# Mamba and additive-attention kernel: one planned order for all engines, built by list scheduling instead of by shares of a phase

## The reference

```python
# 1. mamba, per sample: L = 4096 tokens, 256 inner channels, 16 states
xh, z = split(x @ W_in);  xh = silu(causal_conv_k2(xh));  dt = softplus((xh @ W_x)[:8] @ W_dt + b_dt)
h[t] = exp(dt[t] * A) * h[t-1] + dt[t] * B[t] * xh[t];  y[t] = <h[t], C[t]> + D * xh[t]
x = x + silu(group_norm((y * silu(z)) @ W_out))
# 2. additive attention, causal (strictly below the diagonal), 16 hidden units a
s[i, j] = sum_a w2[a] * tanh(f[i, a] + g[j, a] + b1[a]) + b2;  w = exp(s) masked / its row sum;  t = t + w @ ln(t)
# 3. a layer of 64 experts, each taking its top 8 tokens of a sample out of softmax over tokens of the gate
```

## Time and profile before

| what | us |
|---|---|
| median of 2 runs | 15874.43 (15864.13 to 15884.73) |
| the profiled execution | 15875.92 |
| span of its instructions | 15874.2 |
| first attention tanh starts | 1208.2 |
| one period (sample 4, first exponential of one scan to that of the next) | 1866.5 |

### The profile page before, as it was taken

One profiled execution on the slowest core, in us unless ns is written; L12 is line 12 of the kernel. 1 busy time (PEld: TensorE's weight loads), 2 busy tenths in 40 slices (PEclk: granted clock), 3 DMA queues, 4 the chain that ended last, 5 costly groups with the idle time before them and its releaser, 6 DMA issues.

```text
span 15874.2 us, 128485 instructions
## 1 busy us (share of the span) xinstructions
PE 10063.1 (63%) x51338; PEld 3010.7 (19%) x51338; DVE 8213.9 (52%) x10768; ACT 9981.7 (63%) x6475; POOL 443.8 (3%) x536
## 2 busy tenths in 40 slices
PE   2126556766667666676667666676666766677775
PEld 0001111211122111221122211221112211122223
DVE  5763556355554555455554555645555455542133
ACT  1114566566766666566675666666675766788991
POOL 0000000000000000000000000000000000000000
PEclk6558788888888888888888888888888888889996
DMA  4541554134422445134441344314442244400005
GB/s 147 173 145 68 141 130 120 45 119 125 129 80 76 118 121 126 55 100 114 123 113 41 112 124 125 88 69 114 123 129 65 90 112 123 122 21 32 22 15 195
DMA packets 551062, 1624.30 MB, mean 102 GB/s; under 512 B 49272, under 2 KB 49920, under 8 KB 547904
## 3 DMA queue, kind: packets, MB, share of 16 engines
q1 hardware_dynamic: 550464, 1616.08, 35.4%
HBM read 1368.44 MB, written 247.46 MB: 102 GB/s over the span
## 4 chain that ended last, share of the span: by engine, by line
DMA 28%; PE 27%; ACT 26%; DVE 12%; issue 4%; SPq 2%; POOL 1%; DVEq 0%; POOLq 0%; ACTq 0%
ACT arena L1333 19%; DMA arena<-dt_scratch 17%; PE banks L710 14%; DMA arena<-dx_scratch 8%; PE banks L729 4%; DVE arena L978 3%; ACT arena L1341 3%; ACT arena L1350 2%; ACT arena L1312 2%; DVE arena L1116 1%; PE banks L645 1%; PE banks L741 1%; PE banks L657 1%; PE banks L605 1%; PE banks L686 1%
## 5 line engine op out<-in xcount | busy, mean ns | idle before, releaser
L710 PE MATMUL banks<-arena,w2b 128*32 128x512 f32 (+4 forms) x36864 | 6541.0, 649 | 3707.3 <-ACT arena L1333 2073.8
L1333 ACT ACTIVATE arena<-arena 128x2048 f32<-128x2048 f32 (+15 forms) x4096 | 7011.7, 1785 | 329.5 <-PE banks L710 274.5
L1312 ACT ACTIVATE arena<-arena,An 128x1024 f32<-128x1024 f32 x1024 | 1173.0, 1146 | 3341.3 <-DMA arena<-dt_scratch 3340.4
L710 PEld LDWEIGHTS banks<-arena,w2b 128*32 128x32 f32 x36864 | 1600.5, 122 | 8378.3 <-ACT arena L1333 4255.8
L978 DVE TENSOR_TENSOR_SCAN arena<-arena 128x1024 f32<-128x1024 f32 x1024 | 2386.2, 2330 | 0.0
L969 DVE TENSOR_TENSOR arena<-arena 128x1024 f32<-128x1024 f32 x1024 | 1251.2, 1222 | 1684.1 <-DMA arena<-dx_scratch 1683.0
L1130 DVE TENSOR_TENSOR arena<-arena,banks 128x512 f32<-128x512 f32 (+1 forms) x512 | 334.2, 653 | 2331.2 <-PE banks L729 2331.1
L645 PE MATMUL banks<-arena,sel 128*32 128x512 f32 x4096 | 761.1, 682 | 921.1 <-DVE arena L992 731.1
L992 DVE TENSOR_TENSOR arena<-arena 128x1024 f32<-128x1024 f32 x1024 | 1232.5, 1204 | 152.3 <-DMA arena<-bc_scratch 152.3
L729 PE MATMUL banks<-arena 128*128 128x512 f32 (+3 forms) x2304 | 1080.0, 590 | 70.8 <-POOL arena L1408 31.5
L1341 ACT ACTIVATE arena<-arena 128x1024 f32<-128x1024 f32 (+7 forms) x512 | 1058.3, 2117 | 90.6 <-DVE arena L1116 88.8
(11 more groups left out here) (169 smaller groups left out, 5127.5 us busy)
## 6 DMA issues: line engine op xcount, KB each, us to landing
arena<-dt_scratch SPq DMA_DIRECT2D x1024, 512.0 KB
arena<-dx_scratch SPq DMA_DIRECT2D x1024, 512.0 KB
xc_scratch<-arena SPq DMA_DIRECT2D x64, 512.0 KB, 2.7
gate_scratch<-arena SPq DMA_DIRECT2D x64, 512.0 KB, 2.8
mc_scratch<-arena SPq DMA_DIRECT2D x64, 512.0 KB, 2.9
arena<-mc_scratch SPq DMA_DIRECT2D x64, 512.0 KB, 3.6
arena<-xc_scratch SPq DMA_DIRECT2D x64, 512.0 KB, 5.1
dt_scratch<-arena SPq DMA_DIRECT2D x64, 512.0 KB, 3.0
```

What stands on the lines that cost most here:

```text
L710: mm = e.matmul(TR[32 * q:32 * q + 32, c - sh, l - 512 * c:512], w2b[:, m, :], tile[:, l - org:512 * c + 512 - org], start=(m == 0), stop= ...
L1312: e.activation(DTR[w % NDT], DTR[w % NDT], ACT.Exp, scale=An[:, g:g + 1]).then_inc(decay.h, decay.tick(tuple(k)))
L1333: e.activation(TH[plan.slot[key][q]][:, lo:SUP], Fq[:, I * SUP + lo:I * SUP + SUP], ACT.Tanh, bias=gcol(b, jb, 4 * q + m)).then_inc(tanh.h ...
```

## The change

`BANKS`, the cost lists (`conv`, `scan`, `norm`, `prologue`, `epilogue`, `gate` as lists), `side`, `placed`, `ready`, `room` and the weights are gone. In their place:

- Every step belongs to one engine (`ENGINE`). Steps that had work of several engines are split: `av` (PE) and `avv` (DVE), `d2`, `d2v` and `d2n`, `p1` and `p1v`, and so on. Pairs of halves are split too (`x1`, `x2`, `x3`, `z1` to `z3`, `d2` each with h), and `p3` became `p3g` and `p3f` with `p4g` and `p4f`.
- Steps stand in 16 streams. Within a stream the order is fixed; each step names the steps that it needs, some with a lag.
- `TOOK` and `took` give each step a duration. `LAND` (6.5 us) is the lag between the end of `r` and `q`, one more for `u`; `v0` has 6.0.
- `run` is a list scheduler: it takes the engine that can start soonest, and there the step of the lowest `RANK` among those whose inputs are there (the tanh of attention has the highest number, 5; `S`, `ex`, `F`, `avv` 0; `q` 1; `y` 2; all else 3), and counts the engine's clock on. Banks 5 to 7 go to the one that is free first.
- The tail's order and the arithmetic are the same. `x3`, `x2`, `z1` and the like wait for halves one by one. SyncE's issues are tied to the new names (`x3` with h 1, `d1v`, `e1v`, `e3v`, `e4v`).

The core of the diff (the waits and operands of the other engine functions change only in names and in the split of halves):

```diff
--- before.py
+++ after.py
+    ENGINE = {}
+    for _engine, _ops in (
+            ("ACT", "T T4 ex x2 z2 d3 l1 q t2a G1a"),
+            ("DVE", "F avv dnv x0 x3 z3 d1v d2v d2n d4 k1 u h c k v1 mov g1 g2v t1 t2 p1v p2v p3v p4g p4f f2v f3 e0v "
+                    "e1v e2v e3v e4a e4v G0 G1 G1b G1c G1d G3v G4"),
+            ("PE", "S av dn x1 z1 d1 d2 y mo g2 p1 p2 p3g p3f f1 f2 e0 e1 e2 e3 e4 G2 G3"),
+            ("SP", "k0 r B C v0")):
+        for _op in _ops.split():
+            ENGINE[_op] = _engine
+    TOOK = {"x2": 0.7, "z2": 0.62, "d3": 1.1, "l1": 10.5, "q": 1.16, "t2a": 0.65, "G1a": 3.8, "avv": 0.72, "dnv": 0.75,
+            "x0": 0.1, "x3": 1.15, "z3": 0.76, "d1v": 0.72, "d2v": 0.77, "d2n": 2.0, "d4": 3.25, "k1": 2.5, "u": 1.24,
+            "h": 2.36, "c": 1.22, "k": 0.16, "v1": 1.5, "mov": 1.42, "g1": 0.9, "g2v": 3.0, "t1": 0.56, "t2": 1.5,
+            "p1v": 1.85, "p2v": 1.65, "p3v": 0.72, "p4g": 1.45, "p4f": 0.77, "f2v": 0.72, "f3": 0.77, "e0v": 0.4,
+            "e1v": 1.45, "e2v": 1.85, "e3v": 1.65, "e4a": 0.72, "e4v": 0.77, "G0": 4.6, "G1": 2.5, "G1b": 4.4,
+            "G1c": 4.4, "G1d": 4.7, "G3v": 0.72, "G4": 0.5, "x1": 2.1, "z1": 1.05, "d1": 2.1, "d2": 1.05, "y": 2.1,
+            "mo": 2.1, "g2": 0.3, "p1": 1.1, "p2": 1.1, "p3g": 1.05, "p3f": 1.05, "f1": 1.1, "f2": 1.05, "e0": 2.5,
+            "e1": 1.1, "e2": 1.1, "e3": 1.1, "e4": 1.05, "G2": 1.1, "G3": 2.5, "k0": 1.2, "r": 1.3, "B": 0.7, "C": 0.7,
+            "v0": 2.4, "dn": 2.3}
...
+    RANK = {"S": 0, "ex": 0, "F": 0, "avv": 0, "dnv": 0, "q": 1, "av": 1, "dn": 1, "y": 2, "T": 5, "T4": 5}
+    LAND, SEM = 6.5, 0.15
...
+        self.needs, self.ends, self.clock = {}, {}, dict.fromkeys(("ACT", "DVE", "PE", "SP"), 0.0)
+        streams = {n: [] for n in ("T", "F", "S", "ex", "av", "avv", "conv", "low", "soft", "r", "q", "scan", "y", "v",
+                                   "norm", "side")}
+        self.streams = streams
+        for b in range(NB):
+            self.mamba(b)
         for b in range(NB):
             self.attention(b, 1)
             self.attention(b, 0)
+        self.sides()
+        self.run()
         self.tail()
+
+    def add(self, stream, op, *k, after=()):
+        st = (op, *k)
+        assert st not in self.needs, st
...
+    def mamba(self, b):
...
+        add("r", "B", b, 0, after=[(("k1", b, 7), 3.5), ("z3", b, 7, 1)])
+        add("r", "C", b, 0, after=[("B", b, 0)])
+        for w in range(n):
+            if w % NG32 == 0 and w:
+                add("r", "B", b, w // NG32, after=[("u", b, w - NG32 - 1)] if w > NG32 else [])
+            if w % NG32 == 4 and w > NG32:
+                add("r", "C", b, w // NG32, after=[("c", b, w - 5)])
+            add("r", "r", b, w, after=([("h", b, w - NDT)] if w >= NDT else []) + (
+                [("y", b, (w - NDX) // 2)] if w >= NDX else []))
+            add("q", "q", b, w, after=[(("r", b, w), self.LAND)])
+        for w in range(-1, n + 1):
+            if 0 <= w < n:
+                add("scan", "h", b, w, after=[("u", b, w), ("q", b, w)])
+            if w + 1 < n:
+                add("scan", "u", b, w + 1, after=[(("r", b, w + 1), self.LAND + 1)] + (
+                    [(("B", b, (w + 1) // NG32), self.LAND)] if (w + 1) % NG32 == 0 else []))
+            if w > 0:
+                add("scan", "c", b, w - 1, after=[("h", b, w - 1)] + (
+                    [(("C", b, (w - 1) // NG32), self.LAND)] if (w - 1) % NG32 == 0 else []))
+            if 0 <= w < n - NG32:
+                add("scan", "k", b, w, after=[("h", b, w)])
...
+                    add("v", "mo", b, u // 4, s, after=[("v1", b, u)] + (
+                        [("p1", b - 1, 3), (("t2", b - 1, 7), 4.0)] if b and u == 3 else []))
...
+    def attention(self, b, I):
+        add = self.add
+        ready = [("p4f", b, 4 * I + kk) if 4 * I + kk else ("f3", b) for kk in range(4)]
+        for jb in range(16 * (I + 1)):
+            cs = max(0, jb * 128 - I * SUP)
+            w = SUP - cs
+            g = [("p4g", b, jb // 4)]
+            for m in range(4):
+                key = (b, I, jb, m)
+                self.slots(key, w)
+                free = [("S", *k) if k else None for k in self.slot_before[key]]
+                if w > 1024:
+                    tanhs = [add("T", "T", *key, q, after=ready + g + [f for f in free[q:q + 1] if f])
+                             for q in range(4)]
+                else:
+                    add("F", "F", *key, after=ready + g + [f for f in free if f])
+                    tanhs = [add("T", "T4", *key, after=[("F", *key)])]
+                old = []
+                if m == 0:
+                    self.half_before[key] = list(self.half)
+                    sh = 1024 if self.shifted(jb, cs) else 0
+                    old = [("ex", *self.half[h]) for h in range((cs - sh) // 1024, (SUP - sh) // 1024) if self.half[h]]
+                add("S", "S", *key, after=tanhs + old)
+            self.exp(b, I, jb, cs)
...
+    def bank_for(self, st):
+
+        if st[0] == "y":
+            if st[2] % 4:
+                return 5, 0.0
+            return self.emptied(5)
+        found = [self.emptied(i) for i in self.misc]
+        found = [f for f in found if f]
+        return min(found, key=lambda f: f[1]) if found else None
+
+    def emptied(self, i):
+        c = self.closer.get(i)
+        if c is None:
+            return i, 0.0
+        return (i, self.ends[c] + self.SEM) if c in self.ends else None
+
+    def run(self):
+        heads = {n: 0 for n in self.streams}
+        left = sum(len(x) for x in self.streams.values())
+        while left:
+            found = {}
+            for name, todo in self.streams.items():
+                if heads[name] == len(todo):
+                    continue
+                st = todo[heads[name]]
+                at = 0.0
+                for dep, late in self.needs[st]:
+                    if dep not in self.ends:
+                        break
+                    at = max(at, self.ends[dep] + late)
+                else:
+                    if st[0] in self.EMPTIES or st[0] == "y":
+                        bank = self.bank_for(st)
+                        if bank is None:
+                            continue
+                        at = max(at, bank[1])
+                    found.setdefault(self.ENGINE[st[0]], []).append((at, self.RANK.get(st[0], 3), name, st))
+            assert found, [todo[heads[n]] for n, todo in self.streams.items() if heads[n] < len(todo)]
+            start = {e: max(self.clock[e], min(f[0] for f in c)) for e, c in found.items()}
+            engine = min(start, key=lambda e: start[e])
+            able = [f for f in found[engine] if f[0] <= start[engine] + 0.01]
+            _, _, name, st = min(able, key=lambda f: (f[1], f[0]))
+            heads[name] += 1
+            left -= 1
+            self.put(st, start[engine])
+            self.clock[engine] = self.ends[st]
...
+        self.ends[st] = start + self.took(op, *k)
...
                              stop=True).then_inc(f.h, f.tick(u))
-                elif op == "p3":
+                elif op in ("p3g", "p3f"):
                     evacuated(q_, "p2", *k)
-                    for h, wt in enumerate((W1g, W1f) if k[1] else (W1g,)):
-                        i, f, u = opened((op, *k, h))
-                        e.matmul(TR[:, i, :], wt[:, :, :].rearrange("p a b -> p (a b)"), EPb, start=True,
-                                 stop=True).then_inc(f.h, f.tick(u))
+                    i, f, u = opened((op, *k))
+                    e.matmul(TR[:, i, :], (W1g if op == "p3g" else W1f)[:, :, :].rearrange("p a b -> p (a b)"), EPb,
+                             start=True, stop=True).then_inc(f.h, f.tick(u))
...
-                elif op == "x1" and k[1] < 7:
-                    b, t = k
+                elif op == "x1" and k[1] < 7 and k[2] == 0:
+                    b, t, _ = k
                     if t:
                         written(q_, "z1", b, t - 1, 1)
...
-                elif op == "p4":
+                elif op == "p4g":
...
+                elif op == "p4f":
+                    b, kk = k
+                    i, f, u = full(("p3f", *k))
+                    if b:
+                        q_.wait_ge(tanh, last_tanh(b - 1, 1 if kk >= 4 else 0))
+                    e.tensor_scalar(Fq[:, chunk(kk)], TR[:, i, :], b1r[:, 0:1], None, ALU.add).then_inc(f.h, f.tick(u))
```

644 lines of the change are left out of this document (308 added, 336 removed).

## The result

The changed kernel takes 12862.84 us (median of 2 runs, 12785.72 to 12939.96), 0.8103 of before, 95% interval 0.7893 to 0.8313. The forecast was 14,330 and its range began at 12,900. The direction and the kind of gain were right; the gain is nearly twice as large as forecast (3012 us against 1544). The two runs lie on either side of the range's lower end. The profiled execution is the one of 12939.96 us.

The account below looks back on a forecast made before the run. The prediction took ACT as the engine to keep full and the scan stage as close to bound by its own loads. Its sum 1175 + 7 x 1657 + 1200 + 355 = 14329 gave 14330 us, range 12,900 to 15,400.

Parts of the forecast that it names:

- period: From one sample's first exponential to the next's: 1244 us ACT work + 319 waiting for dt + 94 hand-overs = 1657, against 1866.5.
- last attention: Attention with no mamba beside it: the planner fills ACT, 1200 us instead of 1293, bounds 1170 to 1293.
- The waits of conv and norm: ACT steps of conv and norm listed before their inputs are there: 173.6 us a period, forecast to go.
- The hand-overs: ACT's waits between tanh, S and the exponential of attention: 93.5 us a period, left as is, bounds 30 and 160.
- what the order does to the scan: Scan beside attention: loads nearly never idle, ACT waits for dt 1100 - 781 = 319 us a period instead of 355.7.
- The 1100: Scan stretch beside attention in us, taken near 1216.6 x 0.46 / 0.525 = 1066; the other end was 1217.
- the first rival: Scan loads fall into the fast pace more often: scan 860, dt wait 80, period 1418, total 12,660 us; chance 0.15.
- The 781: The plan's own scan in us, paced by DVE at 6.1 us a group; bounds 5.3 and 7 a group.
- The start: Up to the first tanh: lone scan stays about 860 us, prologue starts beside norm; 1175 instead of 1208, bounds 1130 and 1215.
- Mostly given back: Rival: gain in conv and hand-overs mostly lost, scan stays 1217, period 1840, total 15,610 us, or 15,100 with half; chance 0.19.
- The loads were never the bound: Rival: a group's loads take 5.3 us, the 355.7 us dt wait goes, period 1338, total 12,100 us; chance 0.03.
- The slower case: Rival: each scan exponential comes early, ACT stands 5.1 us each time, total 16,600 us; chance 0.05.

Follow-up runs that it names:

- run 8: Changed kernel planned with a load pair taking 6.8 us of the queue instead of 1.3, landing 4.5 us later instead of 6.5; 12252.19 us, 0.7787 of before.
- run 9: Changed kernel planned with k1 lag 15.0 us instead of 8.0: 12746.6 us, 0.8098; lag 18.0 plus loads over 16 DMA engines: 11718.29 us, 0.7460.
- run 7: Changed kernel with SP waiting before each pair of scan loads until the pair before has landed; 16862.5 us in one run, 1.074 of before.
- run 5: Changed kernel with scan partitions ordered (state, channel), loads over 16 DMA engines: 11825.39 us, 0.7510; the same edit in the kernel before: 14296.03 us, 0.9081.
- run 6: Scan loads alone, all computation left out, plain or with six unequal small transfers ahead; 24 loads took 104.82 us plain, 69.39 us with them.

## Why the prediction was wrong

By its own sum, with the profiled execution's numbers. The period is the mean of seven, (11479 - 1105.5) / 7.

| term | forecast | measured | x | difference |
|---|---|---|---|---|
| first tanh | 1175 | 1105.5 | 1 | -70 |
| period | 1657 | 1482 | 7 | -1225 |
| last attention | 1200 | 1106 | 1 | -94 |
| tail | 355 | 353 | 1 | -2 |

**What was right.** ACT is the engine to count by: work of a period 1244 forecast, 1234.5 measured. The waits of conv and norm go (forecast 0, measured 0.7 of 173.6). The hand-overs stay (94 forecast; 1476 - 1234.5 - 155.9 = 85.6 measured), though by luck: one wait of 52.8 us (runs 8 and 9) makes most of them, and the small ones shrank. The differences of the table add up to -1391 us, from 14329 to the span of 12938; the period makes 88% of them. The wait for dt is still ACT's largest, and the tail is as it was. Of the signs of being right, the rate came (145 GB/s) and the share of 0.50 did not (0.45).

**The step that failed** is "what the order does to the scan": 1100 - 781 = 319 us of waiting for dt; 155.9 was measured. The form is right, a scan bound by its loads minus the scan that the plan believes in. Both numbers in it were wrong, and both so that the wait came out too long.

*The 1100* came from 1216.6 x 0.46 / 0.525: the loads would fill their pauses, at the mean pace that the earlier trace rows had. The scan took 1030, and not by filling pauses: the share is 0.45. It was the pace, 0.203 us a packet instead of 0.247. The text said that what separates the paces isn't seen in the rows and took the mix as a constant. It is not one: it changed with the order in every one of the seven scans, and the trace of run 7 has it back at the slow pace with the loads held up alone. How the new order makes it faster is open (runs 6 and 7): a queue emptied at every group is enough for slow packets, but the moments with an empty queue do not account for before against after. The faster pace was the first rival, with a chance of 0.15 and the total 12,660.

*The 781* came from VectorE's work per group. It left out that the list has stretches with no scan in them. With the loads nearly out of the way the scan takes about 875 (run 5), and 723 and 743 us in the two samples whose lists have no such long stretches. With both measured numbers the step gives 1030 - 875 = 155, the 155.9 of the trace. With one alone put right it gives 249 or 225.

**The start** was costed as full, "it stays about 860". It is 756 at 192 GB/s, 104 us less, by a change of pace (0.205 to 0.184 us a packet at nearly the same share). That is the whole gain there: outside the scan the start takes 1105.5 - 756 = 349.5 us, and took 1208.2 - 860.5 = 347.7, so the earlier prologue gave nothing.

**The last attention** was read from a wrong window. The 1293 us of the earlier trace rows begin at 14226, while sample 6 still has 89 us of tanh and exponentials to go; the first tanh of sample 7 starts at 14315.2. From there:

```profile
14315.20:15519.00 1203.80, 936.41 (x5915) 332.23 (x5913) 324.01 (x636) 1072.14 (x630) 50.56 (x54) 0.91 0.07 23
```

So before it took 1204 us with 1072 of ACT work, and the forecast of 1200 was in truth no gain. It takes 1106 with 1069.69, the idle part falling from 132 to 36 us. That ACT's idle time there would be small (48 forecast) was right; the work of 1152 was 80 too much. The same 89 us stand twice in the forecast's sum for today, 15921; with 1204 there, and the seven periods at their mean of (14315.2 - 1208.2) / 7 = 1872.4, it comes to 15874, the span.

**The rivals.** "Mostly given back" is excluded by the 0.7 us of conv and norm. "The loads were never the bound" is excluded for this change: it needed a group's loads in 5.3 us, the lone scan takes 756 / 128 = 5.9, and loads over 16 engines take the wait for dt from 155.9 to 33 us. The slower case asked whether early exponentials cost 5.1 us each. They do not: 53 of 128 exponentials wait at all, and the sum is 155.9 us. The range left out just the outer end of the fast pace, where the result lies, 37 us below 12,900; one of its two runs lies inside the range.

On the Trainium skill ("DMA: Bandwidth & Descriptors", section "Rules for kernel authors"): its rule on the slowest dimension was right, and worth more than the forecast made of it. It says to put a dimension whose size is a multiple of 16 outermost. The runs agree: the share goes from 0.50 to 0.98 for the loads alone, and the kernel before gets 9% faster.

## What to carry to other kernels

Where the same transfers show two rates at one DMA share, work out the time of a packet from share and rate before and after, and don't hold the mix constant over a change of order; a queue that will run empty at every load is a warning (run 7). A list scheduler gains only what its prices allow, and a wrong price of a shared resource costs time too: here two prices (run 8) took the time from 0.8103 to 0.7787 of before. When the idle time is the difference of two long durations, the error of both enters in full, so bound each by a measured row.

## What the runs showed of the hardware

- Loads of 8 rows to 128 partitions over 8 DMA engines have two paces, 0.16 to 0.18 us a packet of 4 KB (178 to 187 GB/s) and 0.26 to 0.28 (117 to 126 GB/s). Small transfers of unequal length ahead of them gave the fast one in three of four blocks, and transfers strewn in brought it within the block. Without them it stayed slow for all 24 loads. One row for all, eight rows or a row for each partition makes no difference (304.0 and 305.6 us alone; 125 GB/s tight).
- In the kernel a queue emptied at every group gives 0.25 to 0.26 us a packet, 0.18 and 0.20 without that.
- The number of engines that run together matters: loads alone give 65.5 x 0.08 / 28 = 0.19 us with 2 engines, 0.22 with 4, 0.25 with 8. With 16 engines in a tight block a broadcast has 0.285 us (225 GB/s), as has a load of own rows that is cut the same way (228 GB/s), while 128 own rows in one piece had 0.173 (359 GB/s).
- A load of 0.5 MB that waits for the one before takes 305.6 / 48 = 6.4 us, with outer dimension 16 still 218.8 / 48 = 4.6.
